# Unread matmuls on TensorE in the last 40 tiles of two edge passes of a graph network

## The reference

```python
x = _layernorm(x + L0(...))   # edge MLP on x[dst], x[src]-x[dst]; segment_max over dst
x = _layernorm(x + L1(...))   # mean of edge_attr by src, node MLP
x = _layernorm(x + L2(...))   # see below
x = _layernorm(x + L3(...))   # see below

# L2, the mean layer
msg_sum = segment_sum(feature[src], dst); deg = segment_sum(1, dst)
h = where(deg > 0, msg_sum / max(deg, 1), 0)
ge = relu(h @ W_gc + b_gc); h = h * sum(ge == max(ge))
return h @ W_lin.T + b_lin

# L3, typed attention, 4 heads of 16
a = (kw * qw).sum(-1) * rel_pri[:, etype].T / sqrt(16)
ex = exp(a - segment_max(a, dst)[dst]); alpha = ex / segment_sum(ex, dst)[dst]
h = segment_sum(m * alpha, dst)
return typed_linear(h, Wa, ntype)
```

## Time and profile before

| | us |
|---|---|
| median of 3 runs | 19607.6 (19588.42 to 19612.66) |
| profiled execution, its own time | 19425.3 |
| its span, first to last instruction | 19423.5 |

### The profile page before, as it was taken

How to read it: one execution, slowest core, us unless ns; L and a number is a source line. 1 busy time by engine, 2 the same in 40 slices (tenths; PEclk the granted TensorE clock), 3 DMA queues, 4 the chain that set the end, 5 groups by cost and what they waited for, 6 DMA issues and landing times.

```text
span 19423.5 us, 125968 instructions
## 1 busy us (share of the span) xinstructions
PE 4712.7 (24%) x20806; PEld 3710.9 (19%) x20806; DVE 7110.8 (37%) x16320; ACT 1013.1 (5%) x4397; POOL 13120.1 (68%) x13050
## 2 busy tenths in 40 slices
PE   3221221221666666666510000000032000000002
PEld 2100010000566665566410000000021000000001
DVE  5444444443333433333331111111123444444444
ACT  0000000000000000000000000000022000000000
POOL 4666666667666666666657777777755666666665
PEclk9655555555555555555555555555566555555555
DMA  2222222221333333333211121211123333333332
GB/s 71 76 70 68 69 69 67 66 70 51 93 93 91 91 92 93 92 93 93 71 41 45 47 47 47 47 47 47 45 84 121 97 97 97 95 95 97 97 95 55
DMA packets 1464730, 1467.46 MB, mean 76 GB/s; under 512 B 727134, under 2 KB 1226293, under 8 KB 1464536
## 3 DMA queue, kind: packets, MB, share of 16 engines
q1 hardware_dynamic: 1029704, 830.45, 14.2%
q0 software_dynamic: 416960, 533.81, 12.1%
q10 hardware_dynamic: 18000, 102.41, 1.3%
HBM read 863.04 MB, written 602.69 MB: 75 GB/s over the span
## 4 chain that ended last, share of the span: by engine, by line
issue 31%; another core or an unknown queue 19%; DVE 18%; POOL 17%; PE 10%; DVEq 2%; DMA 2%; ACT 1%; SPq 0%; POOLq 0%; ACTq 0%
POOL gat L643 16%; PE pair L1011 4%; DVE oh_lo L1294 2%; DVE prod L1306 2%; DVE oh_hi L1296 2%; PE bank L1000 2%; DVE cur L1391 1%; DVE run_sb L1661 1%; DMA gat<-tab_t,gi 1%; DVE ar L1684 1%; DVE ag_idx L1310 1%; PE bank L1002 1%; PE bank L988 1%; DVE run_sb L1693 1%
## 5 line engine op out<-in xcount | busy, mean ns | idle before, releaser
L600 POOL DMA_INDIRECT perm<-at,ag_idx x3125 | 3135.3, 1003 | 1575.6 <-issue 937.5
L643 POOL DMA_INDIRECT gat<-tab_b,gi x3125 | 3121.2, 999 | 1588.0 <-issue 968.1
L643 POOL DMA_INDIRECT gat<-tab_x,gi x3125 | 3307.4, 1058 | 1191.1 <-issue 1187.7
L643 POOL DMA_INDIRECT gat<-tab_t,gi x3125 | 3027.8, 969 | 1373.5 <-issue 902.5
L1032 PE MATMUL pair<-ident,tails 128*64 128x128 f32 (+1 forms) x20 | 4.9, 421 | 8795.8 <-DVE tails L1474 4423.6
L1011 PE MATMUL pair<-blk,ohb 128*128 128x65 f32 x7500 | 1765.3, 422 | 12.5 <-DVE ohb L1416 12.3
L1032 PEld LDWEIGHTS pair<-ident,tails 128*64 128x64 f32 (+1 forms) x20 | 3.1, 170 | 8797.5 <-DVE tails L1474 4424.4
L1584 DVE TENSOR_TENSOR run_sb<-p,gat 128x320 f32<-128x320 f32 x625 | 314.9, 504 | 3702.2 <-DMA gat<-tab_x,gi 3691.9
L1011 PEld LDWEIGHTS pair<-blk,ohb 128*128 128x128 f32 x7500 | 1645.8, 329 | 88.0 <-DVE ohb L1416 14.0
L961 PE MATMUL bank<-oh_s,lo_bf 128*128 128x490 bf16 x625 | 368.2, 589 | 3219.1 <-DVE prod L1306 2638.4
L1290 DVE TENSOR_TENSOR oh_s<-iota_bf,st_sh 128x490 bf16<-128x490 bf16 x625 | 417.6, 668 | 1760.3 <-remote 1431.9
(11 more groups left out here) (283 smaller groups left out, 9830.6 us busy)
## 6 DMA issues: line engine op xcount, KB each, us to landing
edge<-start_rows SPq DMA_DIRECT2D x250, 800.0 KB
run<-run_sb SPq DMA_DIRECT2D x250, 800.0 KB
blk<-perm SPq DMA_DIRECT2D x750, 165.0 KB
run<-run_sb SPq DMA_DIRECT2D x125, 900.0 KB
at<-in_edge_attr SPq DMA_DIRECT2D x625, 160.0 KB
start_rows<-zeros ACTq DMA_DIRECT2D x125, 800.0 KB
tab_t<-trow SPq DMA_DIRECT2D x98, 512.0 KB
perm<-at,ag_idx POOLq DMA_INDIRECT x3125
```

What stands on the lines that cost most here:

```text
L600: pool.indirect_dma_start(perm_d, rows(perm_d, ag_idx[tp][:, k, s:s + 1]), at[tp][:, s, k, :], None).then_inc(a_sc[tp], 16)
L643: pool.indirect_dma_start(gat[:, k, s, 0:width], None, table, rows(table, gi[tp][:, s, k:k + 1])).then_inc(g_in[k], 16)
```

## The change

TensorE's program gets a helper, and two calls of it: one ahead of `carry` of the mean layer, with the semaphore `c_s`, and one ahead of `carry` of the attention layer, with `d_acc`. The helper loops over the last 40 tiles of the pass. For each group it waits until the groups before it are done (the value is t * 5 + k, so 425 for the first and 624 for the last) and then runs 26 matmuls of 512 columns with bf16 operands into `bank[3]`. Nothing reads their result. That is 200 waits and 5200 matmuls for each pass.

```diff
             last.then_inc(a_hist, 1)
             pe.wait_ge(a_done, 1)
 
+            def keep_warm(groups_done):
+
+                with loop(pe, T - 40, T, 1) as t:
+                    for k in range(KS):
+                        pe.wait_ge(groups_done, t * KS + k)
+                        for _ in range(26):
+                            pe.matmul(bank[3][:, 0:512], zero_bf[:], up_bf[:].unsqueeze(1).broadcast_to([P, 4, P]),
+                                      start=True, stop=True)
+
             def rows_T(t, tp, k, early):
...
                 last.then_inc(n_m["1"], 1)
 
+            keep_warm(c_s)
             carry(1, F, 1)
...
                         products2(b + 2)
 
+            keep_warm(d_acc)
             carry(2, H * HR, 2)
```

## The result

The changed kernel takes 21262.4 us (median of 4 runs, 21240.7 to 21306.8), the kernel before, timed beside it, 19606.3 us (4 runs, 19588.4 to 19612.7). The ratio is 1.0849, interval 1.0828 to 1.0871: slower by 1656 us, where 1 us had been forecast. The profiled execution took 21282.8 us.

What follows compares the result with a forecast made beforehand. GpSimd's gathers were taken to pace both passes. Mean pass 0, attention pass + 2.1 - 1.0 = + 1.1 us, added to the median of 19607.6 us, gave about 19609 us, range 19570 to 19665 us.

Steps and rivals of the forecast that it cites:

- What bounds the kernel: Mean and attention passes: GpSimd's gathers pace both, 7.0 us a group, and nobody there waits for TensorE.
- Do they fit?: TensorE in both passes: 26 matmuls take 5.6 us at the higher clock, at most 6.9, within a group's 7.0 us.
- Other traffic: Both passes: the matmuls add no DMA and do not slow GpSimd's gathers; taken as zero.
- Which clock do they get?: TensorE in both passes: the clock rises to the higher level within a few groups; TensorE is then 80% busy.
- Who waits for them?: Pass ends: only `carry` stands behind the matmuls; mean pass costs nothing, attention pass 2.1 us.
- the cover of 6.5 us: Mean pass end: transposes back end at 14226.0, VectorE goes on only at 14232.49, so lateness up to 6.5 us is hidden.
- the wait of 2.1 us: Attention pass end: the ten transposes, ready at 19146.5, wait 2.1 us for the last 26 matmuls.
- What does the clock give back?: Attention pass end: `carry`'s ten transposes, 2.35 us, shrink by about 1.0 us at the higher clock.
- The second: Both passes: clock stays at the lower level, `carry` comes 820 us late in each, about 21240 us; chance 0.05.
- The third rival: Both passes: matmuls disturb gathers, VectorE's reads or instruction supply by 1 or 2%, 19640 to 19665 us; chance 0.08.
- The first rival: Node stages: the higher clock outlasts the pass and they run warm, priced at 15 us, 19593 us; chance 0.06.
- The range: Whole kernel: 19570 to 19665 us, taking in a 25 us stall either way, run spread and parts of the rivals.

Runs made afterwards that it cites:

- thirty_two: The changed kernel with 32 matmuls of 512 columns behind each group in both passes, not 26: 17217.08 us, kernel before on the same chip 16985.35.
- after_timed: The changed kernel itself, unaltered, timed in 10 runs: 16995.05 us, kernel before on the same chip 16993.94; ratio 1.0001.
- cols128: The changed kernel with its 26 matmuls a group 128 columns wide, not 512, in both passes: 16996.16 us, again 17000.65; kernel before 16989.38 and 16993.94.
- pause_two: The changed kernel with GpSimd pausing each group of the mean pass and 2 matmuls a group in the attention pass: 20784.97 us, kernel before 19652.03.

## Why the prediction was wrong

- **What bounds the kernel**: right; after the change, too, GpSimd's gathers pace both passes, and a group of the mean pass takes 7.0 us.
- ***Do they fit?*** is the step that failed. The spacing of the matmuls was taken as half of 0.43 us, 5.6 us for 26, with 0.265 us as the upper end. Measured in the mean pass: 0.22 us from the rise of the clock to the 44th, then 2.79 us for the next 510, so that 540 of 5200 were done in time. The two rows that bounded it are spacings of TensorE from other stages, and nothing in them covers an instruction that doesn't reach the engine. The upper end should have come from the mean pass's own condition, for which no row had a TensorE instruction; there the prediction had no bound, and said it had one. On a quick chip the step holds: 5.8 us for 26, 6.3 for a group.
- ***Other traffic*** asked only what the matmuls do to the gathers, and there zero is right, on quick chips (thirty_two) and on the slow one (996 gathers in 1399 us, 998 before). It didn't ask what may hold up the matmuls. A hint was there: a gather takes 1058 ns in the mean pass, with TensorE empty, against 999 ns in the max pass with TensorE busy. The prediction used this to say that the matmuls do no harm, and not to ask why GpSimd's issuing is slower where it has the core to itself. The max pass was no proof that TensorE is free beside gathers: its 2986 gathers in 4500 us are one in 1.51 us, the mean pass's 998 in 1399 us one in 1.40 us. That a limit lies between the two would be a guess made afterwards; no run moved the pace in small steps.
- ***Which clock do they get?*** The clock rose as described (at 12970 us, within the first group's matmuls), stayed up on the quick chips through both passes (0.95 and 0.94), and fell on the slow chip behind the first gaps, when little work reached TensorE.
- ***Who waits for them?*** was right in who and in price: the delay of `carry`'s transposes goes into the time one for one. On a quick chip the mean layer costs nothing and the attention layer 2.1 us, to a tenth of a microsecond as forecast. On the slow chip the cover of 6.5 us and the wait of 2.1 us played no part.
- ***What does the clock give back?*** About 1.1 us was found, 1.0 forecast: the ten transposes take 1.25 us, not 2.35. The granted clock over them is 1.00. That goes against the sentence from TensorE: Matmul & The Clock Gate, Part 4 of the Trainium skill; the trace decides. In all after_timed stands 1.1 us above the kernel before, and 1.1 was the sum; the interval of that ratio (17 us each way) is wider, so it is the two terms in the trace that speak for it, and that the totals agree is luck.
- **The rivals.** The second came out near the measured time, 820 us late a pass and 21240 us in all, and had the threshold, 0.269 us. The total is luck, for its cause was wrong: not the clock but a pace of the instructions that the clock doesn't explain, so in the mean pass 1036 us and in the attention pass 640. Its chance, 0.05, was set by doubts about the clock alone. It should have been about *anything* that brings the spacing over 0.269 us, and would have been larger. The third rival named instruction supply, which no run here rules out, but priced it at 1 or 2% of the passes, where what was late was a queue of 5200 instructions. The first rival (warm node stages) gave nothing: from the last transposes of tails to the end it is 277.4 us with the change and 276.9 before on the slow chip, and on quick chips 191.2 us in after_timed and 192.3 in cols128, where that 1.1 us is the transposes themselves (1.25 us against 2.34).
- **The range** took in stalls of one engine by 25 us and the spread of the runs; it had no place for work that piles up. By its difference the forecast holds on quick chips (1.1 us, not to be told from nothing); on the chip of the first measurement the time lies 1597 us above the upper end.

**What stays open.** Why chips differ, and what holds TensorE's instructions back on the slow ones. For the supply of instructions speaks that 44 matmuls with their loads came without a stall before the first gap, as if from a reserve, that the slow pace outlasts the gathers by 20 us, and that ScalarE too stands still with its input ready. The Trainium skill (Runtime: NRT & Kernel Launch, Instruction fetch mechanics) describes that supply as blocks of 256 instructions that a queue of its own fetches ahead. By that one would expect gaps between blocks, not an instruction per 1.40 us, and the page of the kernel after counts only 69 packets of the kind "instruction" in the whole span; so the trace doesn't bear it out in this form. Against it as the whole cause stands that a pause of GpSimd made TensorE's pace normal. The attention pass on slow chips stays open too: bursts of matmuls at full pace between slow stretches, 2227 or 2847 done at the end, with gathers one in 1.45 us; no run varied that. Nor was it tried what number of matmuls costs nothing in a slow chip's mean pass; at the pace seen, 2.79 us a matmul in groups of 7.0 us, it would be 2 a group. In the attention pass there 2 a group cost nothing (pause_two: transposes 1.4 us behind the pass).

## What to carry to other kernels

Unneeded work on an idle engine is free only while it ends in time, and it is the queue behind it that makes it dear: of 5200 matmuls some 4660 were left at the end of the mean pass, and put 1036 us on the path. Before such work is given a place, ask whether the trace has a row for that engine's instructions beside that very load, and if it has none, cap the number so that even a price many times higher fits (here it was 13 times), or let it stop at the end of the pass. And before an edit is called free or dear, time it on more than one chip: here both answers, +0.01% and +8.5%, came from the same kernel.

## What was not expected of the hardware

- The same kernel takes 16985 to 16997 us on four chips and 19481, 19606 and 19652 us in three measurements elsewhere, and an edit that is worth +0.01% on the one kind (0.9991 to 1.0011) is worth +8.5% on the other.
- On slow chips TensorE got out 142 or 143 instructions beside 143 indirect gathers of GpSimd's in 200 us, with 26 and with 8 matmuls a group alike, and went on in steps of 1.40 and 0.70 us for 20 us behind the last gather.
- In the closing stage on a slow chip ScalarE started 46 us behind the transposes that it waits for; on a quick chip 0.04 us.
- With a pause of 2.8 us in GpSimd's issuing in every group the mean pass was equally long on both kinds of chip (5455 and 5460 us), though it is 4346 to 4351 us on slow and 3914 to 3922 us on quick ones without the pause.
- bf16 matmuls of 512 columns with a weight load each follow each other at 0.216 us at the higher clock (4626 in 1000 us), 32 a group as well as 26.
